# A VectorE accumulator moved from SBUF to a PSUM bank, and the bank's former users moved to three others

## The reference

```
h  = norm(x)
q  = h @ Wq / 8 ; k = ctx @ Wk ; v = ctx @ Wv          # 16 heads of 64
b  = sum_k Wto[k] * relu(dist * Wth[k] + bth[k]) + bto + mask    # 32 terms, for all heads
w  = softmax(q k^T + b) ;  x = x + (w v) @ Wo
x  = x + relu(norm(x) @ Wf1 + bf1) @ Wf2 + bf2          # 512 wide
```

## Time and profile before

| what | value |
|---|---|
| median of 3 runs | 1336.05 us (1334.82 to 1336.67) |
| the profiled execution | 1341.9 us, span 1339.8 us |
| mean granted TensorE clock in it | 0.977 |
| busy: TensorE, VectorE | 1209.8 us, 1210.1 us (90% each) |
| busy: ScalarE, GpSimd | 1062.0 us (79%), 820.1 us (61%) |
| TensorE's weight loads | 999.2 us (75%) |

### The profile page before, as it was taken

How to read it: one execution, slowest core, us unless ns; L and a number is a source line. 1 busy time by engine, 2 the same in 40 slices (tenths; PEclk the granted TensorE clock), 3 DMA queues, 4 the chain that set the end, 5 groups by cost and what they waited for, 6 DMA issues and landing times. The chain is left out here.

```text
span 1339.8 us, 36502 instructions
## 1 busy us (share of the span) xinstructions
PE 1209.8 (90%) x11184; PEld 999.2 (75%) x11184; DVE 1210.1 (90%) x4800; ACT 1062.0 (79%) x3353; POOL 820.1 (61%) x828
## 2 busy tenths in 40 slices
PE   1599999999999999999999999999999999799897
PEld 1377878787878787878787877788787878576665
DVE  5999999999999999999999999999999987579996
ACT  4588888888888888888888888888887866478896
POOL 4677777777777777767777777777676743111110
PEclk8699999999999999999999999999999999789998
DMA  6000000001100000011000000110000000000000
GB/s 189 17 1 17 2 18 2 17 18 48 35 17 2 18 2 16 4 57 43 10 9 10 9 10 10 50 49 2 18 2 26 1 2 4 0 10 14 17 12 9
DMA packets 32320, 26.67 MB, mean 20 GB/s; under 512 B 6648, under 2 KB 27008, under 8 KB 32128
## 3 DMA queue, kind: packets, MB, share of 16 engines
q1 hardware_dynamic: 32128, 24.35, 6.3%
HBM read 23.29 MB, written 1.05 MB: 18 GB/s over the span
## 5 line engine op out<-in xcount | busy, mean ns | idle before, releaser
L758 ACT ACTIVATE prob<-score,nmax 128x128 f32<-128x128 f32 x1024 | 397.1, 391 | 121.4 <-DVE nmax L953 121.4
L1358 POOL TENSOR_TENSOR prob<-prob,rinv 128x512 f32<-128x512 f32 x256 | 312.6, 1221 | 274.6 <-DVE rinv L961 273.5
L906 DVE SCALAR_TENSOR_TENSOR bias_acc<-relu_z,cst_all,bias_acc 128x512 f32<-128x512 f32 x370 | 349.8, 945 | 6.6 <-ACT relu_z L741 3.0
L741 ACT ACTIVATE relu_z<-dist_g,cst_all 128x512 f32<-128x512 f32 x386 | 295.6, 806 | 12.9 <-DMA dist_g<-in_fside_BxSxS 10.2
L953 DVE CUSTOM_DVE_ANT_0 score<-L,bias 128x128 f32<-128x128 f32 x1024 | 232.2, 280 | 3.5 <-PE L L484 2.5
L758 ACT ACTIVATION_READ_ACCUMULATOR prob<-score,nmax 128x1 f32 x1024 | 193.9, 189 | 0.0
L494 PE MATMUL T<-ident,prob 128*128 128x128 f32 x1024 | 158.8, 278 | 2.7 <-POOL prob L1358 2.6
L508 PEld LDWEIGHTS O<-probT,v 128*64 128x64 f32 x2048 | 109.7, 136 | 59.8 <-issue 52.1
L484 PE MATMUL L<-kT,qT 64*128 64x128 f32 x2048 | 149.7, 286 | 0.0
L622 PEld LDWEIGHTS M<-wo,oT 128*128 128x128 f32 x1024 | 124.1, 192 | 30.8 <-issue 29.8
L516 PE MATMUL M<-hT,wq 128*128 128x128 f32 x1024 | 127.5, 278 | 20.6 <-DVE v L1063 20.4
(11 more groups left out here) (134 smaller groups left out, 2123.9 us busy)
## 6 DMA issues: line engine op xcount, KB each, us to landing
dist_g<-in_fside_BxSxS SPq DMA_DIRECT2D x16, 256.0 KB, 2.9
mask_g<-in_mask_Bx1x1xS_ff SPq DMA_DIRECT2D x16, 256.0 KB, 3.1
wk<-in_L_xattn_Wk SPq DMA_DIRECT2D x4, 512.0 KB, 3.5
wv<-in_L_xattn_Wv SPq DMA_DIRECT2D x4, 512.0 KB, 3.5
wq<-in_L_xattn_Wq SPq DMA_DIRECT2D x4, 512.0 KB, 3.7
wo<-in_L_xattn_Wo SPq DMA_DIRECT2D x4, 512.0 KB, 4.2
wf<-in_L_xattn_Wf SPq DMA_DIRECT2D x8, 256.0 KB, 2.8
xr<-in_x SPq DMA_DIRECT2D x16, 64.0 KB, 2.2
```

Source lines behind the costliest of these rows:

```text
L741: nc.scalar.activation(relu_z[:, z_slot(g, k), :], dist_g[:, :, :], ACT.Relu, bias=cst(g, C_BTH + k), scale=cst(g, C_WTH + k)).then_inc(z_ ...
L758: last = nc.scalar.activation(prob[:, c, m, :], score[:, c, m, :], ACT.Exp, bias=nmax[:, c, m:m + 1], scale=-1.0, accum_out=rsum[:, c, m:m ...
L906: vec.scalar_tensor_tensor(out=bias_acc[:, :], in0=relu_z[:, z_slot(g, k), :], scalar=weight, in1=bias_acc[:, :], op0=ALU.mult, op1=ALU.ad ...
L1358: gp.tensor_tensor(prob[:, c, :, :], prob[:, c, :, :], rinv[:, c, :].rearrange("p (m o) -> p m o", o=1).broadcast_to([P, 4, P]), ALU.mult) ...
```

## The change

`bias_acc` is no longer a tile of SBUF but the bank M2. All that used M2 in part one goes elsewhere: the transpose of `h2` to T1, the transpose of `h` and f2 to T0, wo to M1. The orders change with it. On TensorE f2 now stands before the apply of quads 2 and 3, and scores 1 before the turn of quad 0, which waits for the sum after f2; wo waits for the copy of v that empties M1, and the second half of the queries for the sum after wo. On VectorE the sum after f2 stands before terms 1. In part two the first transpose into M2 waits for the last bias.

```
+        bias_acc = M2
@@ queries, second half
+                    wait(pe, resid1, after(g, i - 2, 1))
                     pe.wait_ge(v_kept[0], after(g, i, 1))
@@ TensorE, step
-                    wait(pe, resid1, after(g, i - 2, 1))
-                    nc.tensor.transpose(M2[:, 0:P], h2[:, i % 2, :], ident[:, :]).then_inc(h2T_done, 1)
+                    if prev:
+                        pe.wait_ge(pT_odd, after(g, i - 1, 2, 0))
+                    nc.tensor.transpose(T[1][:, 0:P], h2[:, i % 2, :], ident[:, :]).then_inc(h2T_done, 1)
...
-                    wait(pe, h2T_kept, after(g, i - 2, 1))
-                    nc.tensor.transpose(M2[:, 0:P], h[:, (i + 1) % 2, :], ident[:, :]).then_inc(hT_done, 1)
+                    wait(pe, pT_even, after(g, i - 1, 2, 1))
+                    nc.tensor.transpose(T[0][:, 0:P], h[:, (i + 1) % 2, :], ident[:, :]).then_inc(hT_done, 1)
                     keys(g, i + 1, 1)
                     values(g, i + 1, 0)
-                if prev:
-                    apply(g, i - 1, 1)
                 if old:
                     pe.wait_ge(hid_kept, after(g, i - 2, 1))
...
                     for c in range(FILT // P):
-                        last = mm(M2[:, 0:P], hid[:, i % 2, c, :], wf2[:, c, :], start=c == 0, stop=c == FILT // P - 1)
+                        last = mm(T[0][:, 0:P], hid[:, i % 2, c, :], wf2[:, c, :], start=c == 0, stop=c == FILT // P - 1)
                     last.then_inc(f2_done, 1)
-                if cur:
+                if prev:
+                    apply(g, i - 1, 1)
+                if cur:
+                    scores(g, i, 1)
+                    if old:
+                        pe.wait_ge(resid2, after(g, i - 2, 1))
                     turn(g, i, 0)
-                    scores(g, i, 1)
...
                     if nxt:
-                        pe.wait_ge(hT_kept, after(g, i + 1, 1))
-                    wait(pe, resid2, after(g, i - 2, 1))
+                        pe.wait_ge(v_kept[0], after(g, i + 1, 1))
                     for j in range(PAIRS):
-                        last = mm(M2[:, 0:P], oT[:, (i - 1) % 2, j, :], wo[:, j, :], start=j == 0, stop=j == PAIRS - 1)
+                        last = mm(M1[:, 0:P], oT[:, (i - 1) % 2, j, :], wo[:, j, :], start=j == 0, stop=j == PAIRS - 1)
@@ VectorE, step
-                terms(g, i, 1)
                 if old:
                     dve.wait_ge(f2_done, after(g, i - 2, 1))
                     dve.wait_ge(xb_done, after(g, i - 2, 1))
-                    vec.tensor_tensor(x_of(g, i - 2), M2[:, 0:P], xb[:, i % 2, :], ALU.add).then_inc(resid2, 1)
+                    vec.tensor_tensor(x_of(g, i - 2), T[0][:, 0:P], xb[:, i % 2, :], ALU.add).then_inc(resid2, 1)
+                terms(g, i, 1)
```

More of the change, by code:

```diff
@@ L159, in block_program @@
         pool_acc = sb("pool_acc", [P, GROUP, P])
-        bias_acc = sb("bias_acc", [P, GROUP * P])
         bias = sb("bias", [P, GROUP, P])
@@ L557, in step @@
                     pe.wait_ge(h_done[1], after(g, i - 2, 1))
-                    wait(pe, resid1, after(g, i - 2, 1))
[L560 to L563, removed]
-                    nc.tensor.transpose(M2[:, 0:P], h2[:, i % 2, :], ident[:, :]).then_inc(h2T_done, 1)
+                    if prev:
+                        pe.wait_ge(pT_odd, after(g, i - 1, 2, 0))
+                    else:
+                        pe.wait_ge(fT_kept, 2)
+                    nc.tensor.transpose(T[1][:, 0:P], h2[:, i % 2, :], ident[:, :]).then_inc(h2T_done, 1)
                 if cur:
@@ L602, in step @@
                         pe.wait_ge(hT_kept, after(g, i + 1, 1))
+                    elif prev:
+                        pe.wait_ge(pT_even, after(g, i - 1, 2, 1))
+                    else:
+                        pe.wait_ge(fT_kept, 1)
                     for c in range(FILT // P):
-                        last = mm(M2[:, 0:P], hid[:, i % 2, c, :], wf2[:, c, :], start=c == 0, stop=c == FILT // P - 1)
+                        last = mm(T[0][:, 0:P], hid[:, i % 2, c, :], wf2[:, c, :], start=c == 0, stop=c == FILT // P - 1)
                     last.then_inc(f2_done, 1)
+                if prev:
+                    apply(g, i - 1, 1)
                 if cur:
+                    scores(g, i, 1)
+                    if old:
+                        pe.wait_ge(resid2, after(g, i - 2, 1))
+                    else:
+                        pe.wait_ge(hT_kept, after(g, i + 1, 1))
                     turn(g, i, 0)
-                    scores(g, i, 1)
                 if nxt:
@@ L650, in f_turn @@
                 wait(pe, fT_kept, after(g, i, 4, c - 2))
+                if (g, i) == (0, 0) and c % 2 == 0:
+                    pe.wait_ge(resid2, UNITS - 1 if c == 0 else UNITS)
                 for j in range(ROW_HEADS):
@@ L671, in f_step @@
                     pe.wait_ge(fh, after(g, i + 1, 1))
[L673 to L676, removed]
+                    if g == 0 and i == -1:
+                        pe.wait_ge(bias_done, GROUPS)
                     else:
@@ L688, in f_step @@
                     mm(M2[:, 0:P], wqk[:, P:2 * P], src, start=True, stop=True).then_inc(fk_done, 1)
+                    if g == 0 and i <= 0:
+                        pe.wait_ge(resid1, UNITS + i)
                     mm(M1[:, 0:P + EXPERTS], src, wvg[:, :], start=True, stop=True).then_inc(fv_done, 1)
@@ L1018, in step @@
                     wait(dve, f1_done, after(g, i - 4, 1))
-                    vec.tensor_copy(h2T[:, i % 2, :], M2[:, 0:P]).then_inc(h2T_kept, 1)
+                    vec.tensor_copy(h2T[:, i % 2, :], T[1][:, 0:P]).then_inc(h2T_kept, 1)
                 if cur:
@@ L1037, in step @@
                     wait(dve, q_done, after(g, i - 1, 2, 1))
-                    vec.tensor_copy(hT[:, (i + 1) % 2, :], M2[:, 0:P]).then_inc(hT_kept, 1)
+                    vec.tensor_copy(hT[:, (i + 1) % 2, :], T[0][:, 0:P]).then_inc(hT_kept, 1)
                 if isinstance(g, int) and g == 0 and i <= 0:
@@ L1068, in step @@
                     dve.wait_ge(wo_done, after(g, i - 1, 1))
-                    vec.tensor_tensor(x_of(g, i - 1), M2[:, 0:P], x_of(g, i - 1), ALU.add).then_inc(resid1, 1)
+                    vec.tensor_tensor(x_of(g, i - 1), M1[:, 0:P], x_of(g, i - 1), ALU.add).then_inc(resid1, 1)
                 if cur:
```

## The result

The changed kernel takes 1340.79 us (median of 8 runs, 1337.97 to 1343.34); the kernel before, on the same chip in 8 runs, 1336.34. The ratio is 1.0037 with a 95% interval of 1.0023 to 1.0051: slower by 4.5 us. I had predicted 1374 (1350 to 1394), slower by 38. The sign is right, the size is not: most of the loss did not come, and what came lies nearer to no change at all than to the forecast.

The account below looks back on a forecast made before the run. VectorE was taken as the pace, ScalarE's chain from apply to quad 2 a hair behind. 43 x 1.00 - 15 x 0.25 = +39.2 us, last group +2.5, start -3.3: total +38, so 1374 us, range 1350 to 1394.

Parts of the forecast that it names:

- +1.00 us per ordinary step: Ordinary step, 43 of them: quad 2's reciprocal on VectorE moves from 11.11 to 12.11 us after the h2T copy.
- Both waits named as signs: VectorE's reciprocals wait for exps over 100 us instead of 7.8; ScalarE waits for the apply about 110 instead of 50.
- The sign on the steps, 17.7 to 17.8 us: Sign that the forecast is right: ordinary steps, h2T copy to h2T copy, last 17.7 to 17.8 us instead of 16.75.
- From there to the next h2T copy nothing changes: Stretch behind quad 2's reciprocal: keeps its 5.64 us, 5.72 in the long step, as VectorE's terms already take 0.75.
- The long step: Each fourth step, with one more term, 15 of them: quad 2's reciprocal at 12.3 against 12.56 us, -0.25.
- The start: Seven terms in a row at the kernel's start take 5.5 us instead of 8.80: -3.3 us.
- The last group: Last group of four steps, without terms: three steps up to 0.9 us later, one 0.3, partly covered: +2.5 us.
- The term in PSUM at 0.75: VectorE's accumulating term with the accumulator in PSUM: 0.75 us without contention, against a mean of 945 ns before.
- rival 3: The move doesn't end contention, so only the long step's excess before quad 2 stays: +10 us, 1384; chance 0.08.
- rival 4: Reading and writing one bank makes a VectorE term dear, 945 ns: +39 us, 1413; chance 0.06.
- Rival 1: VectorE's sum bounds the step, ScalarE's chain has slack, 71 us come off until TensorE is dense: some 1275; chance 0.09.
- Rival 2: No change: the microsecond is given back by cheaper terms on the return stretch or f2 overlapping the apply; chance 0.03.

Follow-up runs that it names:

- Experiment 2: Kernel before with one move on TensorE, f2 ahead of the apply of quads 2 and 3: 1380.06 us, ratio 1.0301.
- experiment 1: Changed kernel with the accumulator back in SBUF, new banks and order kept: 1378.37 us, ratio 1.0295.
- experiment 3: Kernel before with VectorE's term beside GpSimd's square root moved behind the two normalisations: 1367.28 us, ratio 1.0205.
- experiment 4: Kernel before with GpSimd's sum xb ahead of its square root instead of behind it: 1322.82 us, ratio 0.9885.
- experiment 8: Kernel before with one ScalarE relu moved behind quad 2's exps: 1333.72 us, ratio 0.9962.
- experiment 7: Changed kernel with TensorE's and VectorE's earlier order around f2, and one ScalarE relu moved behind quad 2's exps: 1273.23 us, ratio 0.9517.

## Why the prediction was wrong in size

- **"f2 starts at 3.77", the v copy "moves from 4.98 to 5.98", "+1.00 us per ordinary step": right in mechanism, a little large.** f2 starts at 3.68, the v copy at 5.87, quad 2's reciprocal at 11.94 for 12.11 forecast: +0.83. Experiment 2 shows this move alone with the same 0.83. The difference, 0.17 x 43 = 7.3 us (6.6 if the first step of each group is counted by itself, whose reciprocal moved by 0.88), is 0.11 up to the v copy and the rest in ScalarE's chain, whose exponentials of quads 1 and 2 are 3.91 apart (3.96 before). Both waits named as signs came: 118.7 us for exponentials, 104.0 for the apply. The sign on the steps, 17.7 to 17.8 us, did not: 17.24.
- **"From there to the next h2T copy nothing changes" is the step that failed.** It cost 0.35 x 58 = 20.3 of the 33 us by which I was off. My reason was: "its three terms take 0.75 already, so the change gives it nothing". The terms did take 0.75, before and after. But I had read contention in VectorE's durations alone, and had written that "a term beside which GpSimd rests is one of the 752 ns kind". GpSimd rests beside only one of the three: the first meets its root, the last its product of quad 3 (635.50, 1.52 us). Where the term started first it was GpSimd that was held, and its rows showed it: a root over two elements per partition that takes 1.10 us, and behind it a sum of the same size on VectorE that takes 0.42 where the reciprocal next to it takes 0.17. Experiments 1, 3 and 4 show both halves.
- **The long step, -0.25 forecast:** -0.69 came. 0.35 of it is the same return stretch; the part ahead of quad 2's reciprocal gave 0.34, so that term of the sum was 0.09 small, 1.4 us in all.
- **The start, -3.3 forecast:** -5.4 came. Seven terms take 5.49 as said (5.5), but instructions ahead of them, terms and normalisations of x, had been held as well: the run of seven begins at 36.38 instead of 37.94. I had counted one row of a stretch.
- **The last group, +2.5 forecast:** its four steps take 62.80 us. The profiled execution of before has 62.99, but its granted clock was halved for part of the fourth (0.50 from 1160 to 1166 us); the kernels of experiments 4 and 8, with the order of before, have 61.9. So +0.9 came.
- **The sum:** 38 - 20.3 - 7.3 - 1.4 - 2.1 - 1.6 = 5.3; measured were 4.45, with an interval of 3.1 to 6.8.
- **The term in PSUM at 0.75, and rivals 3 and 4:** 754 ns in the median. Reading and writing the same bank adds 2 ns (rival 4 falls), and no term is above 757 (rival 3 falls). The Trainium skill's SBUF — State Buffer (Who interferes with whom) agrees, and so does its sentence "Issue order, not op shape, decides who blocks": of the two terms of 2.74 us in the earlier trace rows, the first (1.56 us) began behind GpSimd's sum in the earlier trace rows and the second (1.14 us) behind its next product, while the one of 0.75 beside the root began ahead of it. I had used the page's rule for the one side and not for the other. The 65 ns more for PSUM that I had estimated from the Trainium skill's VectorE: DVE Perf Modes (The TRN2 errata) the trace doesn't show: 754 against 752 ns.
- **Rival 1 (1275, "faster by VectorE's pace")** got 0.09 and its reasoning was right on what the freed time is worth: 1273 in experiment 7, with TensorE dense, once the order of before is kept and ScalarE gives 0.71. In the change as made, its condition, slack at the v copy, was missing. **Rival 2 (no change)** has the number nearest to what came and named the return stretch, but by cheaper terms on it, which there aren't.

## What to carry to other kernels

Where two engines share access to a memory, read the durations of both against their own undisturbed value; the instruction that starts first looks clean, and its cost stands in the other engine's row, often in a tiny one on the way back to the head of the loop. When a change relieves a resource and moves an order for it, run the two apart: here one was worth -38 us and the other +42 to +44. And when one engine has been freed, try again the small edits that gave nothing before, as the relu whose gain went from 5 us or less to 23.

## What the runs showed of the hardware

- A VectorE `scalar_tensor_tensor` of 128x512 that accumulates in place in PSUM takes 754 ns (739 to 757), from SBUF 752 when undisturbed and up to 1647 beside GpSimd.
- An operation of 128x2 is held too: GpSimd's root goes from 0.71 to 1.10 us beside a term, and VectorE's sde, with one tensor input, from 0.16 to 0.42 beside an xb of 0.45 that started 0.06 ahead of it, but not beside one that started 0.37 ahead.
- GpSimd's operations of 128x512 show it as well: its product of prob has a mean of 1041 ns with the accumulator in PSUM and 1223 in experiment 1; the one of quad 3 takes 1.04 us instead of 1.52.
